# Products with the values turned: probabilities as weights, two columns of ones, division with queries on the partitions

## The reference

```python
y = roll(layernorm(x), (-4, -4)); windows of 8 x 8, N = 64 tokens
qkv = y @ qkv_w.T + qkv_b
attn = einsum('bhnd,bhmd->bhnm', q * hd ** -0.5, k) + mask
attn = softmax(attn)
out = einsum('bhnm,bhmd->bnhd', attn, v).reshape(-1, N, C)
out = out @ proj_w.T + proj_b
x = shortcut + roll_back(out)
x = x + (gelu(layernorm(x) @ mlp_w1.T + mlp_b1) @ mlp_w2.T + mlp_b2)
x = x * rsqrt(einsum(x * x, gamma_eff) + beta_eff)
```

## Time and profile before

| | |
|---|---|
| median of 3 runs | 1967.57 (1967.16 to 1968.66) |
| the profiled execution | 1966.06, its span 1964.3 |
| PE busy | 1899.8 (97%) |
| DVE, ACT, POOL busy | 1691.6, 1670.0, 1639.8 (86, 85, 83%) |
| granted clock of TensorE, mean | 0.994 |
| a round in the steady part | 14.65 |

### The profile page before, as it was taken

One profiled execution on the slowest core, in us unless ns is written; L12 is line 12 of the kernel. 1 busy time (PEld: TensorE's weight loads), 2 busy tenths in 40 slices (PEclk: granted clock), 3 DMA queues, 4 the chain that ended last, 5 costly groups with the idle time before them and its releaser, 6 DMA issues.

```text
span 1964.3 us, 70181 instructions
## 1 busy us (share of the span) xinstructions
PE 1899.8 (97%) x26628; PEld 1334.7 (68%) x26628; DVE 1691.6 (86%) x4521; ACT 1670.0 (85%) x2968; POOL 1639.8 (83%) x1800
## 2 busy tenths in 40 slices
PE   3899999999999999999999999999999999999995
PEld 2567777777677767777777677777776777667763
DVE  6789898899889888888899898889888899889872
ACT  4788888888888888888888888888888888888886
POOL 2588888888888888888888888888888888888886
PEclk9999999999999999999999999999999999999997
DMA  2222222222222222222222222222222222222110
GB/s 48 37 41 43 42 50 42 42 50 45 39 50 43 41 49 42 43 50 39 45 50 43 42 49 43 41 50 43 41 51 41 42 50 44 41 49 42 34 30 25
DMA packets 217316, 85.01 MB, mean 43 GB/s; under 512 B 117287, under 2 KB 215913, under 8 KB 216985
## 3 DMA queue, kind: packets, MB, share of 16 engines
q1 hardware_dynamic: 216856, 80.33, 21.2%
q0 software_dynamic: 128, 0.20, 0.0%
HBM read 28.03 MB, written 25.17 MB: 27 GB/s over the span
## 4 chain that ended last, share of the span: by engine, by line
PE 95%; DVE 1%; ACT 1%; issue 1%; SPq 1%; POOL 1%; DMA 0%; ACTq 0%; POOLq 0%; DVEq 0%
PE mm_bank L802 48%; PE score_banks L849 10%; PE probs_t_bank L860 9%; PE pv_bank L874 6%; PE mm_bank L884 6%; PE turn_bank L795 6%; PE mm_bank L831 5%; PE turn_bank L788 4%; SPq L319 0%; ACT L573 0%; DVE y_tok L668 0%; DVE shifted L703 0%; ACT L558 0%; DVE row_max L695 0%; SPq L363 0%
## 5 line engine op out<-in xcount | busy, mean ns | idle before, releaser
L418 POOL TENSOR_TENSOR hidden_lo<-hidden,hidden_hi 128x512 fp32r<-128x512 f32 x384 | 487.7, 1284 | 0.0
L695 DVE TENSOR_REDUCE row_max<-score_banks 128x12 f32<-128x768 f32 x256 | 243.7, 952 | 125.5 <-PE score_banks L849 125.5
L668 DVE TENSOR_SCALAR y_tok<-turn_bank,moments,rstd 128x96 f32<-128x96 f32 x1024 | 303.4, 368 | 7.7 <-ACT rstd L484 7.7
L519 ACT ACTIVATE probs_t<-probs_t_bank 128x384 f32<-128x384 f32 x512 | 249.7, 488 | 55.5 <-PE probs_t_bank L860 48.9
L540 ACT ACTIVATE hidden<-mm_bank 128x512 f32<-128x512 f32 x384 | 229.8, 598 | 65.6 <-PE mm_bank L802 50.7
L860 PE MATMUL probs_t_bank<-ident_sb,probs 128*128 128x128 f32 x1536 | 258.9, 277 | 4.0 <-ACT probs_t L519 3.9
L860 PEld LDWEIGHTS probs_t_bank<-ident_sb,probs 128*128 128x128 f32 x1536 | 189.0, 140 | 99.3 <-issue 38.8
L703 DVE TENSOR_TENSOR shifted<-score_banks,row_max 128x768 f32<-128x768 f32 x256 | 245.2, 958 | 8.5
L513 ACT ACTIVATE probs<-shifted 128x768 f32<-128x768 f32 x256 | 214.9, 839 | 27.1 <-DVE shifted L703 26.4
L413 POOL TENSOR_SCALAR hidden_hi<-hidden 128x512 fp32r<-128x512 f32 x384 | 232.7, 617 | 1.8 <-ACT hidden L540 1.8
L849 PE MATMUL score_banks<-k_block,q 64*64 64x192 f32 x4096 | 226.2, 336 | 3.8 <-DMA k_block<-k 2.7
(11 more groups left out here) (115 smaller groups left out, 4752.7 us busy)
## 6 DMA issues: line engine op xcount, KB each, us to landing
x_ext<-in_x SPq DMA_DIRECT2D x128, 192.0 KB, 3.2
k_block<-k SPq DMA_DIRECT2D x768, 32.0 KB, 2.1
out<-o_ext SPq DMA_DIRECT2D x128, 192.0 KB, 2.6
mask_stage<-in_qmask SPq DMA_DIRECT2D x64, 32.0 KB
y_hi<-mask_stage SPq DMA_DIRECT2D x64, 32.0 KB
k_block<-in_kmask POOLq DMA_DIRECT2D x2, 96.0 KB, 4.5
w_raw<-in_w_t SPq DMA_DIRECT2D x1, 144.0 KB
w<-in_w_t SPq DMA_DIRECT2D x1, 144.0 KB
```

The lines of the kernel that those rows point to most:

```text
L418: nc.gpsimd.tensor_tensor(lo, whole, hi, ALU.subtract).then_inc(is_split, 1)
L519: nc.scalar.activation(probs_t[:, a % 2, :, p, :], probs_t_bank[:, 0:HEAD_PAIRS * 128] .rearrange("k (p t) -> k p t", p=HEAD_PAIRS), ACT.C ...
L668: made = nc.vector.tensor_scalar(y_tok[ln][:, c, :], turn_banks[ln][:, n * DIM:(n + 1) * DIM], moments[ln][:, c, 0:1], rstd[ln][:, c:c + 1 ...
L695: nc.vector.tensor_reduce(row_max[:, g, :, :], group_scores(), op=ALU.max, axis=AX.X)\
```

## The change

`v_block` gets two more columns, ones for the rows of either head (`SUMMED` = 34). In `times_v` the turned probabilities are now the weights (128 x 64) and `v_block` is streamed (34 columns); queries come out on the partitions, 64 x 34 for each head pair and window, the last two columns being the two heads' sums. `sum_probs`, `log_sums`, `inverse_sums` and the bank item `sum` are gone. `divide` takes the reciprocal of the sums (24 numbers a partition) and multiplies 384 numbers a partition into `attended_tok`; it stands ahead of `normalise`. PE turns that back in `turn_attended`, four transposes ahead of `turn_probs` 0, into the same bank, and ACT's `attended_copy` brings it to `attended`. MM_ITEMS has nine items in place of ten.

```diff
--- before.py
+++ after.py
@@ -42,6 +42,8 @@
 GROUP_PAIRS = PAIRS // GROUPS
 GROUP = GROUP_PAIRS * HEADS * TOKENS
 CHUNKS = HALF // 128
+VALUES = 2 * HEAD_DIM
+SUMMED = VALUES + 2
 MASK_ROWS = 8
 LN_EPS = 1e-5
 PEDESTAL = 2.0 ** -36
@@ -117,13 +119,13 @@
         q = sb("q", [128, 2, UNIT])
         k = sb("k", [DIM, UNIT])
         k_block = sb("k_block", [128, WINDOWS, TILE_HEADS, TOKENS])
-        v_block = sb("v_block", [128, WINDOWS, HEAD_PAIRS, 32])
+        v_block = sb("v_block", [128, WINDOWS, HEAD_PAIRS, SUMMED])
         row_max = sb("row_max", [128, GROUPS, ROW_TILES, GROUP_PAIRS * TILE_HEADS])
         shifted = sb("shifted", [128, GROUPS, GROUP_PAIRS * TILE_HEADS, ROW_TILES, TOKENS])
         probs = sb("probs", [128, GROUPS, GROUP_PAIRS, TILE_HEADS, ROW_TILES, TOKENS])
         probs_t = sb("probs_t", [128, 2, HEAD_PAIRS, PAIRS, 128])
-        log_sum = sb("log_sum", [DIM, HALF])
-        inv_sum = sb("inv_sum", [DIM, HALF])
+        inv_sum = sb("inv_sum", [128, PAIRS * HEAD_PAIRS, 2])
+        attended_tok = sb("attended_tok", [128, PAIRS, DIM])
         attended = sb("attended", [DIM, HALF])
         attended_hi = sb("attended_hi", [DIM + 1, HALF], f32r)
         attended_lo = sb("attended_lo", [DIM + 1, HALF], f32r)
@@ -185,9 +187,9 @@
         probs_turned = sem("probs_turned")
         probs_t_ready = sem("probs_t_ready")
         pv_made = sem("pv_made")
-        sums_made = sem("sums_made")
-        log_sum_made = sem("log_sum_made")
         inv_sum_ready = sem("inv_sum_ready")
+        divided = sem("divided")
+        attended_turned = sem("attended_turned")
         attended_ready = sem("attended_ready")
         attended_hi_ready = sem("attended_hi_ready")
         attended_split = sem("attended_split")
@@ -244,8 +246,7 @@
 
 
         MM_ITEMS = [
-            ("v", ATTEND, v_ready, 1, 1), ("sum", ATTEND - 1, log_sum_made, 1, 1),
-            ("den", DIVIDE, log_den_made, 1, 1), ("k", QK, k_ready, 1, 1),
+            ("v", ATTEND, v_ready, 1, 1), ("den", DIVIDE, log_den_made, 1, 1), ("k", QK, k_ready, 1, 1),
             ("mlp2", SETTLE, x3_ready, 1, 1), ("q", QK, q_ready, 1, 1), ("proj", PROJECT, x2_ready, 1, 1),
             *((f"mlp1_{n}", MLP, gelu_ready, HID_CHUNKS, n + 1) for n in range(HID_CHUNKS)),
         ]
@@ -521,17 +522,10 @@
                                      .rearrange("k (p t) -> k p t", p=HEAD_PAIRS), ACT.Copy)\
                     .then_inc(probs_t_ready, 1)
 
-            def log_sums(A, a):
-                act.wait_ge(sums_made, A + 1)
-                nc.scalar.activation(log_sum[:, :], mm_bank("sum", a)[0:DIM, :], ACT.Ln)\
-                    .then_inc(log_sum_made, 1)
-
-            def inverse_sums(A, a):
-
-                act.wait_ge(log_sum_made, A + 1)
-                wait(act, attended_ready, A)
-                nc.scalar.activation(inv_sum[:, :], log_sum[:, :], ACT.Exp, scale=-1.0)\
-                    .then_inc(inv_sum_ready, 1)
+            def attended_copy(A, a):
+                act.wait_ge(attended_turned, A + 1)
+                wait(act, attended_split, A)
+                nc.scalar.activation(attended[:, :], pv_bank[0:DIM, :], ACT.Copy).then_inc(attended_ready, 1)
 
             def gelu(A, a, n):
                 if n == 0:
@@ -558,11 +552,10 @@
                 nc.scalar.preload_act_table_set("natural_log_exp_and_others")
                 run(rstd_of, TURN_OUT, 0)
                 run(rstd_of, MLP, 1)
-                run(log_sums, ATTEND - 1)
                 run(softmax_exp, ATTEND, 0)
-                run(inverse_sums, PROJECT)
                 run(log_denominators, DIVIDE)
                 run(k_copy, QK)
+                run(attended_copy, PROJECT)
                 run(probs_t_copy, ATTEND, 0)
                 run(y_copy, TURN_OUT, 0)
                 run(y_copy, MLP, 1)
@@ -603,6 +596,9 @@
             made.then_inc(cleared, 1)
 
             dve.wait_ge(consts_loaded, 16 * CONSTS)
+            nc.vector.tensor_copy(v_block[:, :, :, VALUES:SUMMED].rearrange("k w m e -> k (w m) e"),
+                                  ones_pair_sb[:, :].rearrange("k (e d) -> k e d", e=2)[:, :, 0].unsqueeze(1)
+                                  .broadcast_to([128, WINDOWS * HEAD_PAIRS, 2]))
             head_scale = HEAD_DIM ** -0.5
             def by_tile(row):
                 return row.rearrange("c (r d) -> c r d", r=ROW_TILES)
@@ -706,10 +702,16 @@
                                         ALU.subtract).then_inc(scores_shifted, 1)
 
             def divide(A, a):
+
+                heads = pv_bank[:, 0:PAIRS * HEAD_PAIRS * SUMMED].rearrange("t (i d) -> t i d", d=SUMMED)
+                dve.wait_ge(pv_made, A + 1)
+                nc.vector.reciprocal(inv_sum[:, :, :], heads[:, :, VALUES:SUMMED]).then_inc(inv_sum_ready, 1)
                 dve.wait_ge(inv_sum_ready, A + 1)
-                dve.wait_ge(pv_made, A + 1)
-                nc.vector.tensor_tensor(attended[:, :], pv_bank[0:DIM, :],
-                                        inv_sum[:, :], ALU.mult).then_inc(attended_ready, 1)
+                nc.vector.tensor_tensor(
+                    attended_tok[:, :, :].rearrange("t p (m e d) -> t (p m) e d", m=HEAD_PAIRS, e=2),
+                    heads[:, :, 0:VALUES].rearrange("t i (e d) -> t i e d", e=2),
+                    inv_sum[:, :, :].unsqueeze(3).broadcast_to([128, PAIRS * HEAD_PAIRS, 2, HEAD_DIM]),
+                    ALU.mult).then_inc(divided, 1)
 
             def first_residual(A, a):
                 dve.wait_ge(proj_made, A + 1)
@@ -737,9 +739,9 @@
                 run(max_scores, ATTEND, 0)
                 run(v_blocks, ATTEND)
                 run(shift_scores, ATTEND, 0)
+                run(divide, PROJECT)
                 run(normalise, TURN_OUT, 0)
                 run(normalise, MLP, 1)
-                run(divide, PROJECT)
 
                 run(max_scores, ATTEND, 1)
                 run(shift_scores, ATTEND, 1)
@@ -867,23 +869,22 @@
                 wait(pe, attended_ready, A)
                 pe.wait_ge(probs_t_ready, PAIRS * (A + 1))
                 for p in range(PAIRS):
-                    for n in range(2):
-                        w = (a % 2) * HALF_WINDOWS + 2 * p + n
-                        for m in range(HEAD_PAIRS):
-                            first = (2 * p + n) * TOKENS
-                            made = nc.tensor.matmul(pv_bank[32 * m:32 * m + 32, first:first + TOKENS],
-                                                    v_block[:, w, m, :],
+                    for m in range(HEAD_PAIRS):
+                        for n in range(2):
+                            w = (a % 2) * HALF_WINDOWS + 2 * p + n
+                            first = (p * HEAD_PAIRS + m) * SUMMED
+                            made = nc.tensor.matmul(pv_bank[64 * n:64 * n + 64, first:first + SUMMED],
                                                     probs_t[:, a % 2, m, p, n * TOKENS:(n + 1) * TOKENS],
-                                                    start=True, stop=True)
+                                                    v_block[:, w, m, :], start=True, stop=True)
                 made.then_inc(pv_made, 1)
 
-            def sum_probs(A, a):
-
-                mm_wait("sum", A)
-                for m in range(HEAD_PAIRS):
-                    made = nc.tensor.matmul(mm_bank("sum", a)[32 * m:32 * m + 32, :], ones_pair_sb[:, :],
-                                            probs_t[:, a % 2, m, :, :], start=True, stop=True)
-                made.then_inc(sums_made, 1)
+            def turn_attended(A, a):
+
+                pe.wait_ge(divided, A + 1)
+                for p in range(PAIRS):
+                    made = nc.tensor.transpose(pv_bank[0:DIM, p * 128:(p + 1) * 128],
+                                               attended_tok[:, p, :], ident_sb[:, :])
+                made.then_inc(attended_turned, 1)
 
             def project(A, a):
                 pe.wait_ge(attended_split, A + 1)
@@ -920,13 +921,13 @@
                 run(scores, ATTEND, 0)
                 run(project_v, ATTEND)
                 run(times_v, ATTEND - 1)
-                run(sum_probs, ATTEND - 1)
 
                 run(denominators, DIVIDE)
                 run(project_k, QK)
 
                 run(scores, ATTEND, 1)
 
+                run(turn_attended, PROJECT)
                 run(turn_probs, ATTEND, 0)
                 run(turn_out, TURN_OUT, 0)
                 run(turn_out, MLP, 1)
```

## The result

The changed kernel takes 2005.26 us (median of 4 runs, 2004.41 to 2006.91) against 1967.37 us (4 runs) beside it: ratio 1.0194, 95% interval 1.0177 to 1.021. The forecast was 2010, range 1985 to 2040. The profiled execution took 2004.55 us.

The account below looks back on a forecast made before the run. PE was taken to bound the kernel (97% busy), with late `normalise` on DVE deciding: 0.74 us later minus 0.40 spare gives 0.34 us a round, times 128 is 43.5 us, so 2010 us, range 1985 to 2040.

Parts of the forecast that it names:

- The mechanism: DVE's longer work ahead of `normalise` makes PE wait before its second four y transposes, lengthening each round by 0.34 us.
- 0.18 of waiting: PE ready for the second four y transposes at 1015.07, `normalise` allowing them at 1015.25: a wait of 0.18 us.
- its sign: Idle of PE or its loads before the second y transposes, released by `y_tok`, 0.1 to 0.3 us in nearly every round.
- The DVE step: Reciprocal 0.20, wait on its result 0.03 and product 0.51 ahead of `normalise`, which ends 0.74 us later (0.66 to 0.82).
- The estimate of 0.3 us: Reciprocal on DVE from 24 x 8 cycles plus fixed cost, some 0.3 us; would add 0.1 us a round, 13 us in all.
- The spare time: `normalise` could end 0.40 us later, and no more, before PE's second four y transposes would wait.
- The turned product: `times_v` on PE: 24 rounds of 56 ns, bound by weight load, 1.48 us in place of 1.76.
- rival that a load covers nothing: `times_v` loads not overlapped, 84 ns a round: PE +0.84 us a round, 107 us more, 2075 us; chance 0.10.
- The change of the array's division: Switch of PE's array division, now between `project_v` and `times_v`: 0.11 us, priced from L884 to L802.
- PE's own sum: PE's work a round: 0.28 us gained on the product, 0.44 added for turning back, +0.16 us net.
- Turning back: Four PE transposes of 128 streamed columns ahead of `turn_probs`, 4 x 0.109 = 0.44 us a round.
- From a round to the whole: 128 rounds x 0.34 us = 43.5 us added to the kernel's time.

Follow-up runs that it names:

- e1: Changed kernel with PE's second four y transposes (MLP half) moved behind the first `mlp_down`; 1962.04 us, 0.9974 of the kernel before.
- e2: Changed kernel without the reciprocal, the product taking a constant written once at the start (a probe, division left out); 1963.91 us, ratio 0.9983.
- e6: Kernel before the change with one unused DVE product of 96 x 384 from PSUM added ahead of `normalise`; 1989.03 us, ratio 1.0097.
- e7: Kernel before the change with two unused DVE products of 96 x 384 from PSUM added ahead of `normalise`; 2040.77 us, ratio 1.0362.
- e5: Changed kernel with 64 columns streamed in every `times_v` product instead of 34, `v_block` padded with zeros; 2007.52 us, ratio 1.0194.
- e3: Changed kernel with `times_v` in four column quarters: 48 products with 128 x 32 weights instead of 24 with 128 x 64; 2046.97 us.
- e9: The kernel of e1 with `times_v` moved behind `denominators` on PE; 1986.38 us, ratio 1.0089.

## Why the prediction was right, point by point

- **The mechanism** was the forecast's: `normalise` late, PE standing before the second y transposes in nearly every round. e1 and e2 take that wait away from two sides, and 43 and 41 us go, more than the 38 us of the whole loss. PE's own longer work is 0.02 us a round, some 3 us, and is more than paid by rounds that are no longer disturbed.
- **The size was reached by two errors that cancel.** The forecast was 0.16 us of PE's own work and 0.18 of waiting, 0.34 in all. Measured are 0.02 and 0.36 (15.035 - 14.672), 0.39 in all. The idle of PE's loads, 0.39 us, lies outside the 0.1 to 0.3 that the prediction named as its sign. What made the sum robust was its statement that DVE decides, whatever the product costs between 31 and 63 ns.
- **The DVE step** was put at 0.74 us and is 0.81. The term mis-sized is the reciprocal: 0.20 forecast from the nearest rows, 298 ns by its group and 0.33 from start to start. The reasoning by elements read was wrong: 24 elements cost more than a read of 96 by another operation (248 ns after, 244 before). The estimate of 0.3 us made from the Trainium skill, "VectorE: DVE Perf Modes", section "Walkthrough: the 8-slice pipeline in each mode", came out; with one size of reciprocal in the runs, they don't show that the repeat count is why. The product is 0.47 from start to start, forecast 0.51. Wait on its own result: 0.03, as forecast.
- **The spare time** of 0.40 us came out three times, read at the start of `mlp_down`, right behind the y transposes: 0.41 us later by 0.81 pushed in the changed kernel, 0.07 by 0.47 in e6, 0.53 by 0.93 in e7. What the expectation of e6 left out is the second place, 0.27 us at `second_residual`, which counts for an addition that stays on DVE.
- **The turned product**: 56 ns a round forecast, 58 measured, and e5 and e3 together show that it is the load. The Trainium skill, "TensorE: Matmul & The Clock Gate", section "LDWEIGHTS (loading the stationary operand)", gives columns / 1.2 in ns, 53 for 64, and the 58 ns fit that; for 32 columns it gives 27, and e3's rounds take 36. The prediction's rival that a load covers nothing (84 ns) did not show: 58 is far below, though both products use all 128 rows. Here the measurement differs from the sentence of the Trainium skill that the prediction gives with it, and decides.
- **The change of the array's division**: 0.11 us forecast; `project_v` to `times_v` goes from 1.515 to 1.628 us of the round, 0.11. The Trainium skill, "TensorEngine Tiling (Array Packing)", section "Key Properties", says that a change of the tiling mode drains the engine; the added 0.11 us fit that, and e9 has 0.22 us for one change more, the first load with it.
- **PE's own sum**: +0.16 a round forecast, +0.02 in e1. `denominators` starts at 3.15 us of the round, 3.38 before: 0.23 gained, near the 0.28 said. Turning back takes 0.48 from start to start, not 0.44. So these two give +0.25, and the rest came from what I put at no cost. From `denominators` to the scores of group 1 it is 1.54 us in place of 1.69: `project_k` no longer waits for `log_sums` to empty its bank (before, its load at 1012.41 comes 0.11 us behind the end of `log_sums`) and follows 0.77 us after `denominators` in place of 0.86, and its first product is 0.05 shorter. `turn_probs` 0 takes 0.06 less, since its first load now runs beside the transposes ahead of it. The last 0.02 were not followed.
- **From a round to the whole**: 0.387 x 127 would be 49 us, and 38 were measured; the forecast of 43 was near for the wrong reason. Before, 15 rounds are long, 10.7 us over the median in all, and PE's loads lack instructions for 5.7 and 5.3 us in `times_v` and `sum_probs`. After, there are 3, 0.9 us in all. That is 10 of the 11 us. Part of it is that the wait for `normalise` takes the stalls up: at the scores of group 1, 8 rounds are still 3.5 us late in all, and by the next first scores 0.9 us are left. The other part shows in e1, which has no such wait and only 6 long rounds of 3.2 us: its round is 0.02 us longer than before and its time 6 us less. Before, 48 pairs of load and product went in 0.90 us, straight behind the 64 of `project_v`; now they take 1.40 us, so PE uses up its instructions more slowly. That this is why fits the packets of e3, but no run varies it alone in this kernel.

## What to carry to other kernels

An engine that bounds the kernel by its share can be handed work at no price and still lose, when the change moves another engine's step ahead of one that the first waits for. So read, for each step that is displaced, how long its reader could wait, not how idle its engine is: here DVE idled 1.0 us a round and had 0.4. Moving the reader behind independent work (one line in e1) gave back all of it and made the change a gain of 0.26%. And where a change makes many short instructions of few, look at how they lie in the round before counting the time that each saves: e3 made the product 0.54 us a round shorter and lost 42 us.

## What the runs showed of the hardware

- Matmul records with 128 x 64 fp32 weights follow one another at 58 ns on each of two column halves, whether 34 or 64 columns are streamed (changed kernel, e5); with 128 x 32 on four quarters and 34 streamed at 36 ns (e3).
- With 96 pairs of load and product of 9 ns each behind 64 of 11 ns (e3), PE stood without instructions some 50 times in `times_v`, for up to 2.3 us. Each of the 54 idle times over 0.9 us ended 1.20 to 1.58 us behind the landing of a 16 KB packet of the instruction queue, and one packet came for every 256 records.
- Behind 11 of these stalls, of 1.39 to 2.27 us, the granted clock fell from the 2.4 GHz to the 1.2 GHz level for 3.4 to 6.8 us (e3); behind others of up to 1.98 us it did not.
- A reciprocal of 24 elements a partition from PSUM takes 298 ns, where a product of 384 takes 558 (changed kernel).
- One more change of the array's division in a round cost 0.22 us, the first load behind it with it (e9 against e1).
